# Window attention of a fused convolution and attention block: row maxima through a transpose and DMA, probabilities computed already turned

## The reference, cut to what matters

```
h = ln(t)
q, k, v = (h @ w + b) split into 12 heads of 8
scores = einsum('nqhd,nkhd->nhqk', q, k) / sqrt(8)
attn = softmax(scores)
o = einsum('nhqk,nkhd->nqhd', attn, v)
t = t + o @ wo + bo
t = t + gelu(ln(t) @ w1 + b1) @ w2 + b2
```

## Time and profile before

| | |
|---|---|
| median of the runs | 6391.85 us |
| the profiled execution | 6406.73 us, span 6404.9 us |
| TensorE matmul busy | 6099.7 us, 95% |
| VectorE, ScalarE, GpSimd busy | 60%, 63%, 58% |
| mean granted clock | 0.987 |

### The profile page before, as it was taken

The page is one execution under the profiler, slowest core; times in us unless marked ns, Lnnn a source line. Parts: engine busy times, 40 slices in busy tenths (PEclk is TensorE's granted clock), DMA queues, the critical chain, the costliest instruction groups (busy, mean ns, idle before and its releaser), DMA issues.

```text
span 6404.9 us, 186325 instructions
## 1 busy us (share of the span) xinstructions
PE 6099.7 (95%) x73264; PEld 4931.2 (77%) x73264; DVE 3871.3 (60%) x6330; ACT 4030.2 (63%) x5970; POOL 3726.4 (58%) x4567
## 2 busy tenths in 40 slices
PE   6999999999699999999999999999999999999998
PEld 6999999999577777777777777777777777777776
DVE  1222222222267777777777777777777777777775
ACT  3434444344367777777777777777777777777776
POOL 2222222222267777777777777777777777777775
PEclk9999999999689999999999999999999999999999
DMA  4434444344245555555555555555555555555553
GB/s 114 109 100 106 110 109 108 101 105 98 59 101 119 121 119 119 118 117 120 119 120 120 119 118 118 118 120 120 120 120 119 118 118 118 119 120 120 120 119 81
DMA packets 1053080, 723.37 MB, mean 113 GB/s; under 512 B 431125, under 2 KB 1024117, under 8 KB 1052117
## 3 DMA queue, kind: packets, MB, share of 16 engines
q1 hardware_dynamic: 1023028, 672.74, 46.3%
q0 software_dynamic: 29184, 38.71, 2.5%
HBM read 401.80 MB, written 309.23 MB: 111 GB/s over the span
## 4 chain that ended last, share of the span: by engine, by line
PE 64%; DVE 5%; issue 4%; ACT 0%; POOL 0%; DVEq 0%; SPq 0%; DMA 0%; POOLq 0%; ACTq 0%
PE ps_pv L1073 13%; PE ps_ring L1014 9%; PE ps_t L1058 9%; PE ps_ring L1137 7%; PE ps_s L1045 6%; PE ps_ring L1128 3%; PE ps_xc L1114 3%; PE ps_ring L1023 3%; PE ps_ring L1099 3%; DVE b_sq_hi L919 2%; PE ps_ring L1031 2%; DVE b_o L939 2%; PE ps_ring L1032 1%; PE ps_ring L1025 1%; PE ps_ring L1024 1%
## 5 line engine op out<-in xcount | busy, mean ns | idle before, releaser
L1073 PEld LDWEIGHTS ps_pv<-b_vd,b_probs_t 128*64 128x64 f32 x24576 | 805.9, 139 | 329.1 <-issue 328.7
L903 DVE TENSOR_REDUCE b_mx<-ps_s 128x12 f32<-128x588 f32 x1024 | 788.6, 770 | 348.0 <-PE ps_s L1045 348.0
L221 POOL TENSOR_SCALAR xn<-xin,aff 96x896 f32<-96x896 f32 x192 | 233.3, 1215 | 1208.1 <-DVE aff L328 1195.4
L1073 PE MATMUL ps_pv<-b_vd,b_probs_t 128*64 128x18 f32 x24576 | 907.8, 214 | 0.1
L796 ACT ACTIVATE b_probs_t<-ps_t 128x588 f32<-128x588 f32 x1024 | 688.1, 672 | 346.7 <-PE ps_t L1058 346.5
L1058 PE MATMUL ps_t<-b_const,b_probs 128*128 128x128 f32 x6144 | 875.4, 279 | 0.6 <-ACT b_probs L805 0.3
L699 POOL TENSOR_TENSOR b_mid_lo<-b_mid,b_mid_hi 128x392 fp32r<-128x392 f32 x768 | 791.3, 1030 | 114.0
L415 PE MATMUL ps_conv<-toep_hi,blocks_hi 128*128 128x304 f32 (+5 forms) x4032 | 844.3, 291 | 0.0
L415 PE MATMUL ps_conv<-toep_hi,blocks_lo 128*128 128x304 f32 (+5 forms) x4032 | 839.5, 290 | 0.0
L415 PE MATMUL ps_conv<-toep_lo,blocks_hi 128*128 128x304 f32 (+5 forms) x4032 | 838.4, 290 | 0.0
L1058 PEld LDWEIGHTS ps_t<-b_const,b_probs 128*128 128x128 f32 x6144 | 700.4, 141 | 123.8 <-issue 91.4
(11 more groups left out here) (141 smaller groups left out, 12699.0 us busy)
## 6 DMA issues: line engine op xcount, KB each, us to landing
stacked_qk<-b_planes SPq DMA_DIRECT2D x3072, 73.5 KB
b_q_st<-stacked_qk SPq DMA_DIRECT2D x256, 441.0 KB, 4.6
b_k_st<-stacked_qk SPq DMA_DIRECT2D x512, 220.5 KB, 5.3
toep<-filters_padded SPq DMA_DIRECT2D x96, 936.5 KB, 6.9
b_xs<-x_scratch SPq DMA_DIRECT2D x224, 147.0 KB, 5.6
out<-b_outs SPq DMA_DIRECT2D x224, 147.0 KB, 5.6
xin<-x SPq DMA_DIRECT2D x96, 336.0 KB
x_scratch<-x1t POOLq DMA_DIRECT2D x96, 336.0 KB, 5.7
```

Source lines behind the costliest of these rows:

```text
L903: dve.tensor_reduce(mx[:, p % 2, :].rearrange("q (g j) -> q g j", g=2), scores, AX.X, ALU.max).then_inc(S["mx_done"], 1)
L1073: ins = pe.matmul(ps_pv[WS * w:WS * w + WS, col:col + 2 * VA], pt[:, p % 2, h, w, :], vd[:, par, 2 * p + w, h, :, :].rearrange("k a d -> k ...
```

## The change

Scores are computed twice. First query-major as before, now with one matmul for each head (`scores`, 24 for each pair of windows, contraction 48, 49 x 49), only for the row maxima. The 48 columns of maxima of a strip (12 heads x 4 pairs) are transposed by one TensorE instruction (`max_rows`), split into three bf16 planes by VectorE and GpSimd, written to DRAM and loaded as rows 48 to 50 behind the stacked q; the rows behind the stacked k hold -1. Then key-major (`below_max`, 24 for each pair, contraction 51): the result is already score minus maximum, turned. ScalarE's exponential reads it from PSUM and writes the weights of `times_v`. Subtraction, transposes and copies (`shift_scores`, `turn`, `turned`) are gone.

The even head of a pair lies on partitions 0 to 50, the odd one on 64 to 114, each with its own PSUM bank. `times_v` takes one head for two windows rather than two heads for one window (same count), in two halves of 48 instructions. v is 8 matmuls of 96 moving columns in place of 16 of 48. The stages become LOAD 0, GN 1, QKV 2, STK 3, ATT 4, MAXR 5, SOFT 6, PROJ 7, MLPS 8, STORE 9, and buffers grow (`xs` 10, stacks 4, `vd` 6 strips). SyncE writes the planes in 6 DMAs with a broadcast source in place of 12, loads the stacks in 4 and the maxima in 2. The low part of h2 moves from GpSimd to VectorE, idle instructions (`settled`) go. In the ring v now comes last, behind w2 and the maxima.

```diff
-    LOAD, GN, QKV, ATT, PROJ, MLPS = 0, 1, 2, 4, 5, 6
-    VR = 4
+    LOAD, GN, QKV, STK, ATT, MAXR, SOFT, PROJ, MLPS, STORE = 0, 1, 2, 3, 4, 5, 6, 7, 8, 9
+    VR, XS, SR = 6, 10, 4
...
                 ("q", QKV, "q_done", 1, 1), ("k", QKV, "k_done", 1, 1), ("var2", PROJ, "lg2", 1, 1),
-                ("v", QKV, "v_done", 1, 1), ("w2", MLPS, "y_done", 1, 1)]
+                ("w2", MLPS, "y_done", 1, 1), ("mt", ATT, "mx_rest", 1, 1), ("v", QKV, "v_done", 1, 1)]
...
+            def put(n, plane, ready):
+                sp.wait_ge(S[ready], n + 1)
+                for side, terms in enumerate((TERMS_Q, TERMS_K)):
+                    at = [j for j in range(NTERM) if terms[j] == plane]
+                    to = slice(at[0], at[-1] + 1, at[1] - at[0] if len(at) > 1 else 1)
+                    sp.dma_start(stk[n % 2, side, :, to, :], planes[:, plane, side, :].unsqueeze(1).broadcast_to(
+                        (C, len(at), NT))).then_inc(stk_written[n % 2], 16)
...
ScalarE:
             def exps(i, m, p):
-                act.wait_ge(S["sub_done"], PAIRS * m + p + 1)
-                after(act, i, "t_ps", PAIRS * m + p - 1)
-                act.activation(probs[:, p % 2, :, 0:TOK], ss[:, p % 2, :, :], ACT.Exp,
-                               scale=float(DH) ** -0.5).then_inc(S["exp_done"], 1)
+                act.wait_ge(S["r_ps"], PAIRS * m + p + 1)
+                after(act, i, "pv_ps", 2 * (m - 1) + 1 + p // 2)
+                act.activation(pt[:, p, 0:HEADS * TOK].rearrange("k (e n) -> k e n", e=2),
+                               ps_t[:, :, 0:HPAIR * TOK], ACT.Exp, scale=float(DH) ** -0.5).then_inc(S["exp_done"], 1)
...
TensorE:
+            def products(dst, a, b, m, p, depth):
+                for h in range(HPAIR):
+                    for e in range(2):
+                        for w in range(2):
+                            k = slice(WS * e, WS * e + depth)
+                            t = slice((2 * p + w) * TOK, (2 * p + w + 1) * TOK)
+                            ins = pe.matmul(dst[WS * w:WS * w + TOK, e, h * TOK:(h + 1) * TOK], a[k, m % SR, h, t],
+                                            b[k, m % SR, h, t], start=True, stop=True, skip_group_check=True)
+                return ins
...
+                after(pe, i, "mx_done", PAIRS * m + p)
+                products(ps_s, q_st, k_st, m, p, SLOT).then_inc(S["s_ps"], 1)
...
+                after(pe, i, "exp_done", PAIRS * m + p)
+                products(ps_t, k_st, q_st, m, p, SLOTM).then_inc(S["r_ps"], 1)
...
VectorE, behind w2's addition:
+                    dve.tensor_tensor(h2_lo[:, :], h2[:, :], h2_hi[:, :].bitcast(F32), ALU.subtract).then_inc(
+                        S["h2_split"], 1)
+                if att is not None:
+                    maxima = bank(i, s, "mt")[0:NMAX, 0:2 * WS].rearrange("r (w t) -> r w t", w=2)[:, :, 0:TOK]
...
+                    dve.tensor_copy(mx_planes[:, 0, :, :], maxima).then_inc(S["mx_high"], 1)
...
+                    dve.tensor_tensor(mx_rest[:, :, :], maxima, mx_planes[:, 0, :, :], ALU.subtract).then_inc(
+                        S["mx_rest"], 1)
```

More of the change, by code:

```diff
@@ L547, in steps @@
                     step(i, s)
-            for s in range(MLPS):
-                step(BATCH, s)
+            for s in range(STORE):
+                step(BATCH + s // B, s % B)
         def after(eng, i, name, count):
@@ L600, in window_pass, with x_landed @@
         NPAR = 19
[L601 to L606, removed]
+        WRITES, LOADS = 16 * 2 * 3, 16 * 4
+        def x_landed(n):
+            return sum(16 if m % B < B - 1 else 32 for m in range(n % XS, n + 1, XS))
         block = ctx.enter_context(nc.Block())
@@ new lines, in step @@
+                n = strip(i, s, STORE)
+                if n is not None:
+                    sp.wait_ge(S["out_done"], n + 1)
+                    sl = n % B
+                    for d, cnt, dst in rows(out, n // B, sl):
+                        sp.dma_start(dst, outs[:, sl % 2, d:d + cnt, 0:HW]).then_inc(stored[sl % 2], 16)
+                n = strip(i, s, STK)
+                if n is not None:
+                    sp.wait_ge(stk_written[n % 2], WRITES * (n // 2 + 1))
+                    after(sp, i, "r_ps", PAIRS * (n - SR + 1))
+                    for side, dst in enumerate((q_st, k_st)):
+                        rows_e = stk[n % 2, side].rearrange("(m r) j t -> (r j) m t", m=HPAIR)
+                        for e in range(2):
+                            sp.dma_start(dst[WS * e:WS * e + SLOT, n % SR, :, :],
+                                         rows_e[SLOT * e:SLOT * e + SLOT]).then_inc(stk_loaded[n % 2], 16)
@@ L649, in step @@
[L649 to L657, removed]
@@ L665, in step @@
[L665 to L670, removed]
+                    put(n, 0, "k_high")
+                    put(n, 1, "rest_high")
             steps(sp, step)
@@ L1062, in times_v @@
-            def times_v(i, par, m, p):
+                pe.matmul(bank(i, s, use)[0:C, 0:NT], ones[:, :], hi[:, :], start=True, stop=False)
+                pe.matmul(bank(i, s, use)[0:C, 0:NT], ones[:, :], lo[:, :], start=False, stop=True).then_inc(S[done], 1)
+            def products(dst, a, b, m, p, depth):
+                for h in range(HPAIR):
+                    for e in range(2):
+                        for w in range(2):
[4 more added lines that the diff above has]
+                return ins
```

413 lines of the change are left out of this document (193 added, 220 removed).

## The result

| | us |
|---|---|
| before, beside it on the same chip | 6391.77 median (6381.32 to 6405.57, 4 runs) |
| after | 6812.24 median (6770.47 to 6860.44, 4 runs) |
| ratio | 1.0659, 95% interval 1.0573 to 1.0745 |
| the profiled execution | span 6858.6 (before 6404.9) |

A forecast was written before the change was run, and what follows sets the result against it. TensorE's program was taken as the bound: 18.06 us a strip falling to 16.66 (15.85 work, 0.71 and 0.10 waits). 6406.7 - 358 + 25 = 6074 profiled, median 6060; range 5800 to 6450.

The forecast's parts named there:

- A granted clock below 1.00 between strips: Listed sign that the forecast is wrong: TensorE's clock under full rate between strips; no size or chance given.
- Small matmuls: TensorE's score groups: 12.5 ns a pair, 0.41 us per group of 24, 3.06 us a strip for eight groups.
- faster tiles: Rival: small score matmuls take 6.1 ns as moving columns halve; period 15.43 us, time 5745; chance 6%.
- rivals with slower pairs: Row halves taking turns, 22.5 ns a pair, 6550 us (17% with like cases); in-between floor, 17.5 ns, 6304 us (16%).
- The new wait of v: TensorE before v, whose bank waits for `y`: 0.71 us idle in every strip.
- Other waits: TensorE ahead of var2, waiting for GpSimd's split of sq2: 0.10 us a strip.
- A wait takes the place: Rival: VectorE or ScalarE comes 0.8 us late at GELU, h1, `y`, maxima or v; period 17.46, 6260 us; 11%.
- v and the rest: TensorE: new v 0.80 us, `times_v` in two groups -0.22; VectorE 11.5 us a strip, ScalarE 10.4.
- Emptying the pipeline: Two more steps fill and empty the pipeline: between nothing and 33 us, taken as +25.

The follow-up runs named there:

- a_fill_hole: Changed kernel plus four unread f32r matmuls (128 rows, 96 weight columns, 288 moving) in TensorE's gap before v: 6291.18 us, ratio 0.9843.
- a_fill_light: Changed kernel plus the same kind of four unread matmuls behind `scores` 0, gap before v left: 6684.25 us, ratio 1.0460.
- a_fill_small: Changed kernel plus 64 of its own small bf16 matmuls in the gap before v, instead of four dense ones: 6459.46 us, ratio 1.0105.
- the split versions: Changed kernel with each `times_v` half cut in two: 7084.44 us; with four gap matmuls too: 6929.59; then also sq2's low part on VectorE: 6920.44.
- the filled kernels: Changed kernel with four dense unread matmuls in the gap before v, alone or with further edits, `times_v` not cut further: 6249.01 to 6301.67 us.
- a_split_fill: Changed kernel with each half of `times_v` cut in two, plus four unread matmuls in the gap before v: 6929.59 us, ratio 1.0838.
- a_fill_dve: Changed kernel plus four unread matmuls in the gap before v, low part of sq2 on VectorE rather than GpSimd: 6273.31 us, ratio 0.9829.

## Why the prediction was wrong

**The step that failed** has no term in the sum. I priced every TensorE instruction at its duration from a stretch with a granted clock of 1.00 and took that clock as given, while 2.86 us of 128 x 128 transposes, the densest work of the step, went out and small matmuls and a gap came in. "A granted clock below 1.00 between strips" stood in the list of what would make the forecast wrong, with no price and no rival. It could have had a price: the page has a 6 in its clock row at the change of passes, and as an estimate a strip wholly at half the clock costs up to its 15.85 us of TensorE's work more. What came is 37% of the time there: a mean strip of 19.4 us has 7.2 us at half speed and would lose 3.6 by it. It lost 2.8 (16.6 to 19.4), among other things because slow strips wait less (1.12 us where those at the full clock wait 1.52) and a small group takes less than double. At the full clock throughout, 255 x (16.6 - 18.11) + 56 + 2 = -327 us would have come, a median near 6065.

That the transposes kept the clock up in the kernel before is shown: taking them out costs it some 530 us, putting other dense work in their place brings 1.00 back. How much of that is the missing work and how much the gaps that it left isn't separated. That the changed kernel's clock answers to added work in the same way is shown by a_fill_hole, a_fill_light and a_fill_small. How rows, columns, busy time and place in the step weigh against each other is open, as is why the split versions fall as far as they do.

**Small matmuls**: 12.5 ns a pair of weight load and matmul were forecast. A group takes 0.27 us in the chain, (0.27 - 0.11) / 24 = 6.7 ns; from start to start it is 7.0. So "faster tiles", to which I gave 6%, was the right size. By the chain, six groups at 0.27 us and two behind another of their kind at 0.21 are 2.04 us where the sum had 3.06: 1.0 too much. The argument against it was that 49 weight columns keep up a tile's rhythm of 45 ns. The starts say 26.5, with 24.5 in the bound for moving columns (20.4 at 2.4 GHz and 4). The slow L1073 was f32 with 128 rows; I carried its rhythm over to bf16 with 48. Both rivals with slower pairs fall.

**The new wait of v**: 0.71 forecast, 0.69 measured. Its place and its cause were right.

**Other waits**: 0.10 forecast for var2; L1023 waits 63.7 / 115 = 0.55 us where it does, 0.33 over all strips. And w1a waits 0.32 for the maxima's rest, which the forecast didn't have: one layer norm lies between v and w1a, VectorE comes to h2's low part and to the maxima only behind `y`, and on that way stands the copy that takes 913 ns instead of 350. "A wait takes the place" was thus right in part. In strips at the full clock the waits are 1.52 us together and TensorE's own time 15.08. By luck, 0.8 us too much for the work (15.85) and 0.7 too little for the waits (0.81) cancel, and 16.60 stands against 16.66.

**v and the rest**: v 0.87 against 0.80; `times_v` 1.51 for 48, just what two groups of 24 and one start give in the sum (2 x 0.70 + 0.11); VectorE 12.4 us a strip and ScalarE 10.8 against 11.5 and 10.4 (over strips of 19.4 us), of which the slow copy is 0.56 for VectorE. **Emptying the pipeline**: +25 forecast, no more than 33 held possible; +56 measured, and still +44 to +54 in the filled kernels. The mean clock over this end is 0.84 before, 0.58 in the changed kernel and 0.60 to 0.66 in the filled ones, so how much is the added steps and how much the clock isn't separated.

## What to carry to other kernels

Where TensorE runs at its full clock, ask of each dense piece of work that is to go whether it keeps the clock: a kernel that is busy over 90% of the time fell to a mean of 0.81 here. Price a forecast for such a change at both levels, and read the clock row of the page before any wait. When it has fallen, a few wide matmuls in gaps where TensorE waits anyway are the cheap remedy (6812 to 6291 us for four a strip), and they also show at once whether the clock is the cause. Where they stand matters: the same four elsewhere brought 128 us, and a reordering meant to spread the light parts cost 272.

## What the hardware showed

- The granted clock fell to half while TensorE was busy 93% of the time, with no wait longer than 0.8 us (mean 0.81 from 2600 to 6300 us).
- On four tiles of 64 x 64, pairs of a 49-column bf16 weight load and matmul start every 7.0 ns (161 ns for 23); one tile by itself starts one every 26.5 ns at the full clock. The Trainium skill, "TensorE: Matmul & The Clock Gate", Wait — 56ns, not 53.3ns?, has matmuls start no closer than about 25 ns; on tiles that work side by side the measurement decides against it, for one tile the trace agrees.
- A group of 24 such pairs costs 0.27 us in the chain at the full clock and 0.39 to 0.41 at half, less than double.
- A copy of 96 x 392 on VectorE, f32 to fp32r, took 350 ns alone and 1020 (median) while GpSimd's L760 ran for more than 0.3 us of it; the overlap explains nearly all of the spread (correlation 0.996 over 190 copies).
- TensorE busy for 96% of a stretch had a granted clock of 0.83 (a_split_fill), busy for 92% one of 0.98 (a_fill_dve).
